# Edge network of one graph layer: the smallest kind of edges multiplied edge by edge in float32 on weights as loaded, placed between the two larger kinds; the second gathered row added one tile behind

## The chip, the core and the metric

The kernel runs on 1 core of one Trainium2 chip. The metric is the time of one execution on the device in microseconds (us). The five engines of the core (TensorE, VectorE, ScalarE, GpSimd, SyncE) run their own instruction lists and meet at semaphores; 16 DMA engines serve all queues of the core.

## What is computed

Two graph layers over 512 nodes with 1024 features, float32. Nearly everything here is in the first one, its edge network:

```python
feat = jnp.concatenate([n_f[edge_src], n_f[edge_dst]], axis=1)      # 8192 edges, 2048 wide
e_hh = jax.nn.relu(feat[:E_HH] @ W_hh + b_hh)                       # 256 edges
e_oo = jax.nn.relu(feat[E_HH:E_HH + E_OO] @ W_oo + b_oo)            # 1280 edges
e_ho = jax.nn.relu(feat[E_HH + E_OO:] @ W_ho + b_ho)                # 6656 edges
logit = (jnp.concatenate([e_hh, e_oo, e_ho], axis=0) @ W_a + b_a)[:, 0]
...                                                                 # alpha: softmax of logit over the edges of a node
z_f = jax.ops.segment_sum(alpha[:, None] * n_f[edge_src], edge_dst, num_segments=N)
h_new = jax.nn.relu(nf2[:NH] @ W_hn + b_hn)                         # nf2 = [n_f, z_f]
o_new = jax.nn.relu(nf2[NH:] @ W_on + b_on)
```

Here n_f is relu(layernorm(x)). The second layer normalizes again, multiplies by W, and sums over neighbours.

## The kernel before

**Tables and tiles.** A row of `feat @ W` is a sum of two rows: source node times the upper half of W, target node times the lower half. So the kernel does not multiply edges. For each of the three kinds of edges (ho, oo, hh, in this order) it multiplies the 512 node rows by both halves of W and stores the results as tables in DRAM, `tab_a` (upper half) and `tab_b` (lower half, bias added). The 8192 edges form 64 tiles of 128: 52 of kind ho (tiles 0 to 51), 10 of oo (52 to 61), 2 of hh (62, 63). For each tile GpSimd gathers 128 rows of 4 KB from `tab_a` and 128 from `tab_b` by an indirect DMA (512 KB each) into slots of `gath` (8 slots). For odd tiles below 62 the two rows go to two slots and VectorE adds them (L888); for all others the second DMA adds onto the first in SBUF (L307), issued `LAG` = 2 tiles behind the first. VectorE then takes relu, times W_a, and the sum of a row in one pass (L893), which frees the slot: this is `edge(q)`.

**Chunks.** TensorE works in chunks of a [1024 x 512] piece of weights: 8 steps k, in each 4 groups of 128 nodes times 3 passes (L638), because a float32 value is held as a high and a low float32r part (`actT_h`, `actT_l`; `ring_h`, `ring_l`) and high*low, low*high, high*high are summed. Chunks 0 to 3 are W_ho, 4 to 7 W_oo, 8 to 11 W_hh (two column halves n for `tab_a`, then two for `tab_b`), 12 to 15 the upper halves of W_on, W_hn, W_hn, W_on over the nodes they concern (3, 1, 1 and 3 groups). A weight tile is loaded by SyncE into one of 8 places of `raw` once VectorE has used the tile there (L232); ScalarE rounds it to `ring_h` (L435), VectorE subtracts for `ring_l` (L868). After a chunk its four banks go to `stage` and to the table: by ScalarE for `tab_a` (L453), by VectorE with the bias for `tab_b` (L876).

**Work hung between the steps.** (c, k) below is step k of chunk c. In chunks 2 to 5 each step also counts two tiles of edges: VectorE makes two one-hot matrices (L819, L820), TensorE multiplies them (L588) into 512 x 512 counts in banks 0 to 3, which ScalarE copies out (L440) at the end of each kind. From chunk 6 on each step adds the logits of a tile: VectorE makes two one-hots (L910, `logit_onehots`), ScalarE scales one by the three bf16 parts of the logit (L482, three instructions a tile, `logit_parts`), TensorE accumulates (L588, three matmuls a tile). A tile takes one of 4 one-hot slots. `SUM_AT` says at which (c, k) tile q is summed: 7 tiles a chunk in chunks 6 to 11, then 8, 6, 6 and 2. `EDGE_AT` puts `edge(q)` 12 steps earlier. When the last tile of a kind is in, the banks are closed (L611), VectorE reads them (`copy_kind`, L932), and the next kind is opened with a mask (L607). Also on VectorE: the inverse counts (L918, L920) in chunks 8 to 10, and the split of finished logits (L899 to L904).

**After chunk 15** come the row maximum (L1006 to L1008), the exponentials, the row sums, the transposes of the attention matrix, the product for z_f (L624), the lower halves of W_hn and W_on, and the second layer. All of that is the same in both kernels.

## Time and profile before

| | us |
|---|---|
| median of 3 runs | 651.68 (649.97 to 654.79) |
| the profiled execution | 648.16 |
| its span in the profile | 646.0 |
| TensorE busy | 556.7 (86%) |
| VectorE busy | 453.9 (70%) |
| ScalarE busy | 306.2 (47%) |
| GpSimd busy | 173.4 (27%) |
| DMA read from and written to HBM | 123.27 MB, 16.78 MB |

The trace of the profiled execution begins 0 us at the start of the span, and all times below are counted from there. A window view gives, for a stretch of the span, how long each engine was busy and in how many instructions, the clock that TensorE was granted, the share of the time in which the 16 DMA engines had a packet in work (it can come out a little over 1), and GB/s. TensorE's busy time in a dense stream overlaps itself, so the distance between starts, not the duration of one matmul, tells its pace.

### The profile page before, as it was taken

The page shows a single profiled execution, that of the slowest core. Times are in us where ns is not written, and L with a number is a line of the kernel's source. Part 1 is how long each engine was busy: PE and PEld are TensorE (multiplying, and loading weights), DVE is VectorE, ACT ScalarE, POOL GpSimd, SP SyncE. Part 2 cuts the span into 40 slices and gives each one's busy share as a digit, 9 for nine tenths or more (in the row PEclk, how much of TensorE's full clock was granted, in tenths as well). Part 3 has the DMA queues.
Part 4 walks back from the last instruction along what each step waited for, and adds up shares of the span by engine and source line. Part 5 has one row for each costly group of instructions (what it writes and reads, how often), then busy time and mean ns, then how long its engine had stood idle before and what let it go on. Part 6 is the DMA issues. An engine that isn't in the chain of part 4 may idle for free.

```text
span 646.0 us, 8205 instructions
## 1 busy us (share of the span) xinstructions
PE 556.7 (86%) x2376; PEld 409.7 (63%) x2377; DVE 453.9 (70%) x958; ACT 306.2 (47%) x485; POOL 173.4 (27%) x165
## 2 busy tenths in 40 slices
PE   0799999999879997979898997568949999779987
PEld 0688777776636765657575764324738788567865
DVE  6715256677986969999989786676795289783252
ACT  2613312114069996656655564499843182332200
POOL 2000300075364564566655553200030000000000
PEclk9999999999979999999998997888978899979999
DMA  8335453499999999999999999843355075130021
GB/s 326 124 132 172 145 192 136 144 243 380 324 331 343 296 328 339 316 330 349 341 342 303 332 317 339 224 145 111 106 225 198 16 245 185 61 102 29 0 82 49
DMA packets 55973, 140.51 MB, mean 218 GB/s; under 512 B 6274, under 2 KB 6402, under 8 KB 55938
## 3 DMA queue, kind: packets, MB, share of 16 engines
q0 software_dynamic: 20624, 74.98, 37.5%
q1 hardware_dynamic: 27072, 50.34, 22.7%
q10 hardware_dynamic: 8242, 14.75, 6.2%
q8 instruction: 18, 0.29, 0.2%
q14 instruction: 17, 0.14, 0.1%
HBM read 123.27 MB, written 16.78 MB: 217 GB/s over the span
## 4 chain that ended last, share of the span: by engine, by line
PE 51%; DVE 22%; DMA 11%; ACT 7%; issue 6%; POOL 2%; ACTq 1%; DVEq 0%; POOLq 0%
PE ps L638 30%; DMA gath<-tab_b,tabl_i 8%; PE ps L624 6%; PE ps L588 4%; ACT onehot L482 4%; DVE gath L893 4%; PE ps L797 3%; DVE gath L888 3%; PE ps L769 3%; DVE ring_l L868 2%; PE ps L782 2%; DVE onehot L910 2%; DMA gath<-tab_a,tabl_i 2%; ACT ring_h L435 1%; DVE logit_d L932 1%
## 5 line engine op out<-in xcount | busy, mean ns | idle before, releaser
L638 PE MATMUL ps<-ring_h,actT_h 128*128 128x512 f32 x520 | 225.8, 434 | 7.2 <-DVE actT_l L861 5.5
L638 PE MATMUL ps<-ring_h,actT_l 128*128 128x512 f32 x520 | 205.5, 395 | 0.0
L638 PE MATMUL ps<-ring_l,actT_h 128*128 128x512 f32 x520 | 204.9, 394 | 0.0
L482 ACT ACTIVATE onehot<-onehot,lgs 128x512 bf16<-128x512 bf16 x192 | 124.6, 712 | 72.3 <-DVE onehot L910 56.4
L435 ACT CAST ring_h<-raw 128x512 fp32r<-128x512 f32 x176 | 104.0, 616 | 105.9 <-PE ps L638 70.7
L868 DVE TENSOR_TENSOR ring_l<-raw,ring_h 128x512 fp32r<-128x512 f32 x176 | 116.9, 685 | 42.0 <-ACT ring_h L435 42.0
L638 PEld LDWEIGHTS ps<-ring_h,actT_h 128*128 128x128 f32 x520 | 99.6, 191 | 41.4 <-DVE actT_l L861 6.5
L588 PE MATMUL ps<-onehot 128*128 128x512 bf16 x292 | 84.1, 398 | 37.3 <-ACT onehot L482 34.2
L638 PEld LDWEIGHTS ps<-ring_h,actT_l 128*128 128x128 f32 x520 | 98.9, 190 | 22.2
L638 PEld LDWEIGHTS ps<-ring_l,actT_h 128*128 128x128 f32 x520 | 99.5, 191 | 20.1
L293 POOL DMA_INDIRECT gath<-tab_a,tabl_i x64 | 69.6, 1088 | 147.9 <-DVE gath L893 69.0
L893 DVE SCALAR_TENSOR_TENSOR gath<-gath,wa_b 128x1024 f32<-128x1024 f32 x64 | 78.4, 1225 | 27.4 <-DMA gath<-tab_b,tabl_i 24.9
L307 POOL DMA_INDIRECT gath<-tab_b,tabl_i x33 | 58.3, 1767 | 64.8 <-DMA tab_b<-stage 47.0
L588 PEld LDWEIGHTS ps<-onehot 128*128 128x128 bf16 x292 | 21.6, 99 | 82.0 <-issue 70.4
L819 DVE TENSOR_SCALAR onehot<-iota_f,node_f 128x512 bf16<-128x512 f16 x64 | 23.4, 366 | 31.9 <-PE ps L588 31.7
L300 POOL DMA_INDIRECT gath<-tab_b,tabl_i x31 | 34.2, 1103 | 24.2 <-DVE gath L893 18.4
L910 DVE TENSOR_SCALAR onehot<-iota_f,node_f 128x512 bf16<-128x512 f16 x128 | 39.4, 350 | 1.1 <-PE ps L588 0.7
L888 DVE TENSOR_TENSOR gath<-gath 128x1024 f32<-128x1024 f32 x31 | 37.7, 1217 | 0.8 <-DMA gath<-tab_b,tabl_i 0.7
L861 DVE TENSOR_TENSOR actT_l<-ps,actT_h 128x512 fp32r<-128x512 f32 x24 | 16.2, 688 | 29.8 <-ACT actT_h L427 29.7
L427 ACT CAST actT_h<-ps 128x512 fp32r<-128x512 f32 x24 | 13.7, 591 | 44.8 <-PE ps L624 34.7
L453 ACT COPY stage<-ps 128x512 f32<-128x512 f32 x24 | 14.1, 586 | 34.4 <-PE ps L638 27.7
L820 DVE TENSOR_SCALAR onehot<-iota_f,node_f 128x512 bf16<-128x512 f16 x64 | 22.2, 348 | 0.0
(162 smaller groups left out, 503.0 us busy)
## 6 DMA issues: line engine op xcount, KB each, us to landing
raw<-in_L_gnn_W_ho_dram SPq DMA_DIRECT2D x32, 256.0 KB
raw<-in_L_gnn_W_oo_dram SPq DMA_DIRECT2D x32, 256.0 KB
...
```

The lines of the kernel that those rows point to most:

```text
L293: pool.indirect_dma_start(out=gath[:, c % GB, :], out_offset=None, in_=tab_a[0:kinds * N, :], in_offset=bass.IndirectOffsetOnAxis(ap=tabl_ ...
L300: pool.indirect_dma_start(out=gath[:, c % GB, :], out_offset=None, in_=tab_b[0:kinds * N, :], in_offset=bass.IndirectOffsetOnAxis(ap=tabl_ ...
L307: pool.indirect_dma_start(out=gath[:, c % GB, :], out_offset=None, in_=tab_b[0:kinds * N, :], in_offset=bass.IndirectOffsetOnAxis(ap=tabl_ ...
L435: nc.scalar.copy(ring_h[:, k, :], raw[:, k % RAW, :]).then_inc(s_high, 1)
L482: ins = nc.scalar.mul(onehot[:, s, 1 + i, :], onehot[:, s, 1, :], lgs[:, i, q:q + 1])
L588: mm = nc.tensor.matmul(ps[:, bass.ds((lo + j) & 3, 1), :].rearrange("p a n -> p (a n)"), onehot[:, s, 1 + i, j * P:(j + 1) * P], onehot[: ...
L624: mm = nc.tensor.matmul(ps[:, b, :], w, v, start=(i == 0), stop=(i == len(pairs) - 1))
L638: mm = nc.tensor.matmul(ps[:, first + m, :], w, v, start=(k == 0 and i == 0), stop=(k == KT - 1 and i == 2))
L868: nc.vector.tensor_tensor(ring_l[:, k, :], raw[:, k % RAW, :], f32(ring_h[:, k, :]), ALU.subtract).then_inc(s_low, 1)
L888: nc.vector.tensor_tensor(gath[:, c % GB, :], gath[:, c % GB, :], gath[:, d % GB, :], ALU.add).then_inc(s_sum, 1)
L893: nc.vector.scalar_tensor_tensor(out=gath[:, c % GB, :], in0=gath[:, c % GB, :], scalar=0.0, in1=wa_b[:, :], op0=ALU.max, op1=ALU.mult, ac ...
L910: ins = nc.vector.tensor_scalar(onehot[:, SLOT[q], j, :], iota_f[:, :], node_f[:, q, e:e + 1], None, ALU.is_equal)
```

## The change

**The hh kind is multiplied by edges.** `KINDS` and the tables of hh are gone. The relu'd rows are stored to a DRAM array `h_d`; four indirect DMAs gather the 2 x 128 source and 2 x 128 target rows of the hh edges from it into `gath`; inside chunk 0 TensorE transposes them (32 transposes, at steps 5 and 7), ScalarE copies them to `featT` (8 copies), which lies over `hrow`; `hrow` is loaded back from `h_d` in chunk 12. Chunks 4 to 7 are now W_hh: at each step two float32 products [128 edges] x [128 x 512], with the weights read straight from `raw`, without rounding, without low part. Both halves of W_hh add up in one bank, so nothing is stored; VectorE adds the bias and takes relu, W_a and the sum from the bank (`hh_edges`, two instructions for each of 4 banks). `raw` is freed by TensorE in these chunks. Chunks 8 to 11 are W_oo.

**The tables of numbers.** Counts begin a chunk earlier, in chunks 1 to 3 (48 tiles), and the last 16 lie in the steps of chunks 4 and 5. Edges: tiles 0 to 11 in chunks 4 to 7, then one at every step of chunks 8 to 12 (tiles 12 to 51), tiles 52 to 58 (oo) from (13, 4) to (15, 2), and 59 to 61 after the last step. Sums: the two hh tiles in chunk 8, 7 tiles in each of chunks 9 to 11, 16 in chunk 12, 8 in 13, 7 in 14, 7 in 15 from step 3 on, 3 after chunk 15. The hh kind is closed first, then ho, then oo. The inverse counts lie in chunks 7, 8 and 10. The seeds of the inverse counts on ScalarE lie in chunks 6 and 7.

**Smaller ones.** `LAG` is 1. The index arithmetic of the edges (VectorE) and its transposes (TensorE) come before chunk 0's products instead of in and after them.

```diff
+        featT = sb("featT", [P, 2 * KT, E_HH], F32, over="hrow")
...
-        tab_a = nc.dram_tensor("tab_a", [3 * N, D], F32).ap()
-        tab_b = nc.dram_tensor("tab_b", [3 * N, D], F32).ap()
+        tab_a = nc.dram_tensor("tab_a", [2 * N, D], F32).ap()
+        tab_b = nc.dram_tensor("tab_b", [2 * N, D], F32).ap()
+        h_d = nc.dram_tensor("h_d", [N, D], F32).ap()
...
+                if q:
+                    if is_split(q - 1):
+                        sp.wait_ge(s_low, RAW + nth_split(q - 1) * KT + k + 1)
+                    else:
+                        sp.wait_ge(s_slot, KT + (q - 1) * KT + k + 1)
+                sp.dma_start(raw[:, k % RAW, :], w[row + k * P:row + (k + 1) * P, n * FB:(n + 1) * FB]).then_inc(s_raw[k % RAW], 16)
...
+            load_chunk(W_ho, 0, 0, 0)
+            for m in range(NM):
+                sp.wait_ge(s_h, m + 1)
+                sp.dma_start(h_d[m * P:(m + 1) * P, :], hrow[:, m, :]).then_inc(s_hd, 16)
+            load_chunk(W_ho, 0, 1, 1)
+            for n in range(NN):
+                load_chunk(W_ho, D, n, 2 + n)
+            for n in range(NN):
+                for half in range(2):
+                    load_chunk(W_hh, half * D, n, CH_HH + 2 * n + half)
+            for half in range(2):
+                for n in range(NN):
+                    load_chunk(W_oo, half * D, n, CH_OO + 2 * half + n)
...
+                if q == CH_EDGE:
+                    sp.wait_ge(s_hd, 16 * NM)
+                    for m in range(NM):
+                        sp.dma_start(hrow[:, m, :], h_d[m * P:(m + 1) * P, :]).then_inc(s_hrow, 16)
...
+            for i in range(2 * T_HH):
+                pool.indirect_dma_start(out=gath[:, NM + i, :], out_offset=None, in_=h_d[:, :],
+                                        in_offset=bass.IndirectOffsetOnAxis(ap=hh_i[:, i:i + 1], axis=0)).then_inc(s_hg[i], 16)
...
-            LAG = 2
+            LAG = 1
...
-        SUM_AT |= {(12, k): 42 + k for k in range(8)}
+        SUMS_AT |= {(12, k): (21 + 2 * k, 22 + 2 * k) for k in range(KT)}
+        LAST_SUMS = (59, 60, 61)
-        EARLIER = 12
+        EDGES_AT |= {(8 + i, k): (12 + i * KT + k,) for i in range(4) for k in range(KT)}
...
+            def hh_rows(j):
+                act.wait_ge(s_ftp, j + 1)
+                nc.scalar.copy(featT[:, 2 * j:2 * j + 2, :].rearrange("p a b -> p (a b)"), ps[:, j % NM, :]).then_inc(s_ft, 1)
...
+            def hh_transposes(k):
+                if k in (5, 7):
+                    if k == 5:
+                        pe.wait_ge(s_spanok, 1)
+                        for i in range(2 * T_HH):
+                            pe.wait_ge(s_hg[i], 16)
+                    for b in range(NM):
+                        j = b + (0 if k == 5 else NM)
+                        if k == 7:
+                            pe.wait_ge(s_ft, b + 1)
+                        for f in (2 * j, 2 * j + 1):
+                            for t in range(T_HH):
+                                c = f % 2 * E_HH + t * P
+                                mm = nc.tensor.transpose(ps[:, b, c:c + P], gath[:, NM + 2 * t + f // KT, f % KT * P:(f % KT + 1) * P], ident[:, :])
+                        mm.then_inc(s_ftp, 1)
+            def hh_chunk(n, half):
+                q = CH_HH + 2 * n + half
+                for k in range(KT):
+                    pe.wait_ge(s_raw[k], 16 * q + 16)
+                    f = half * KT + k
+                    for t in range(T_HH):
+                        b = NM + 2 * n + t
+                        if half == 0 and k == 0:
+                            pe.wait_ge(s_copied, 4 * NM + 2 * n + t + 1)
+                        mm = nc.tensor.matmul(ps[:, b, :], featT[:, f, t * P:(t + 1) * P], raw[:, k, :], start=(f == 0), stop=(f == 2 * KT - 1))
+                        if f == 2 * KT - 1 and t == 0:
+                            mm.then_inc(s_hhc, 1)
+                    mm.then_inc(s_slot, 1)
+                    later_counts(q, k)
...
+            edge_chunk(0, 0, before=hh_transposes)
+            pe.wait_ge(s_ft, KT)
             open_banks()
-            with pe.Fori(0, 3) as c:
-                edge_chunk(c + FIRST_COUNTS, after=lambda k: count_tiles(c * 2, k))
-            edge_chunk(LAST_COUNTS, after=last_counts)
-            pe.wait_ge(s_ccopy, 3)
-            open_masked(0)
-            with pe.Fori(0, 6) as i:
-                edge_chunk(i + 6, before=lambda k: uniform_sums(i, k))
+            with pe.Fori(0, LOOP_COUNTS) as c:
+                edge_chunk(c + FIRST_COUNTS, c + FIRST_COUNTS, after=lambda k: count_tiles(c * 2, k))
+            reg[0] = codes(48 // G, G)
+            for n in range(NN):
+                for half in range(2):
+                    hh_chunk(n, half)
+            chunk(CH_OO, NM, range(NM), lambda m: pe.wait_ge(s_hhd, m + 1), before=lambda k: sums(SUMS_AT.get((CH_OO, k), ())), counted=True)
+            pe.wait_ge(s_kfree, NM)
+            open_masked(0, 2)
+            with pe.Fori(0, 3) as i:
+                edge_chunk(i + CH_OO + 1, i + 5, before=lambda k: uniform_sums(i, k))
...
+            sums(LAST_SUMS)
...
+            def hh_edges(n):
+                dve.wait_ge(s_bias, 48)
+                for t in range(T_HH):
+                    if t == 0:
+                        dve.wait_ge(s_hhc, n + 1)
+                    else:
+                        chunk_done(dve, CH_HH + 2 * n + 1)
+                    b = NM + 2 * n + t
+                    c = slice(n * FB, (n + 1) * FB)
+                    step(nc.vector.tensor_tensor(ps[:, b, :], ps[:, b, :], bias2[:, 0, c], ALU.add))
+                    nc.vector.scalar_tensor_tensor(out=ps[:, b, :], in0=ps[:, b, :], scalar=0.0, in1=wa_b[:, c],
+                                                   op0=ALU.max, op1=ALU.mult, accum_out=lgh[:, t, n:n + 1]).then_inc(s_hhd, 1)
...
+            for p in LAST_EDGES:
+                edge(p)
+            split_logits(LAST_EDGES[0], TG)
+            for p in LAST_SUMS:
+                logit_onehots(p)
+            copy_kind(1)
```

TensorE's rows where the chunks of W_hh end and chunk 8 begins, in the changed kernel (before, chunks 7 and 8 are both made of rows like the last three, 96 to a chunk); L783 are the float32 products:

```order
L688 MATMUL ps<-zeros_r 128x512 x4
L783 MATMUL ps<-raw,featT 128x512 x32
L719 MATMUL ps<-ring_h,actT_h 128x512
L719 MATMUL ps<-ring_l,actT_h 128x512
L719 MATMUL ps<-ring_h,actT_l 128x512
```

The last two chunks of hh are one uninterrupted row of 32 products (64 in the four chunks), where 384 matmuls stood.

ScalarE's rows in chunk 12 before (L435 rounds a weight tile, L482 scales a one-hot, so three of them are a tile):

```order
L435 CAST ring_h<-raw 128x512
L482 ACTIVATE onehot<-onehot,lgs 128x512 x3
L435 CAST ring_h<-raw 128x512
L482 ACTIVATE onehot<-onehot,lgs 128x512 x3
L461 DMA tab_b<-stage 128x512 x4
L435 CAST ring_h<-raw 128x512
L482 ACTIVATE onehot<-onehot,lgs 128x512 x3
```

The same place in the changed kernel, where L500 is the rounding and L547 the scaling, and, behind the dots, its last rows before the exponentials (L610 splits the node rows):

```order
L500 CAST ring_h<-raw 128x512
L526 DMA tab_b<-stage 128x512 x4
L547 ACTIVATE onehot<-onehot,lgs 128x512 x6
L500 CAST ring_h<-raw 128x512
L547 ACTIVATE onehot<-onehot,lgs 128x512 x6
...
L500 CAST ring_h<-raw 128x512
L547 ACTIVATE onehot<-onehot,lgs 128x512 x6
L500 CAST ring_h<-raw 128x512
L547 ACTIVATE onehot<-onehot,lgs 128x512 x18
L610 CAST hrow_h<-hrow 128x1024 x4
```

In chunk 12 two tiles stand between two roundings instead of one, and behind the last rounding of chunk 15 stand six tiles (x18) before the split of the node rows.

GpSimd's rows in the steady part, before (L293 gathers from `tab_a`, L300 from `tab_b` for a plain tile, L307 adds from `tab_b` onto the slot):

```order
L293 DMA gath<-tab_a,tabl_i 128x1024
L300 DMA gath<-tab_b,tabl_i 128x1024
L293 DMA gath<-tab_a,tabl_i 128x1024
L307 DMA gath<-tab_b,tabl_i 128x1024
```

and in the changed kernel (L343, L350, L357 are the same three):

```order
L343 DMA gath<-tab_a,tabl_i 128x1024 x2
L350 DMA gath<-tab_b,tabl_i 128x1024
L357 DMA gath<-tab_b,tabl_i 128x1024
```

The adding DMA of an even tile no longer waits behind the first gather of the next even tile, but stands ahead of it.

## Rows read from the trace of the kernel before

**Rows 1.** Windows: us, busy us of each engine (instructions), TensorE clock, DMA share, GB/s

```profile
core 0: us, PE busy (x) PEld busy (x) DVE busy (x) ACT busy (x) POOL busy (x), PEclk, DMA share, GB/s
47.90:70.50 22.60, 22.60 (x102) 18.27 (x101) 9.90 (x28) 7.10 (x13) 0.00 (x0) 1.00 0.42 141
97.00:123.00 26.00, 26.00 (x116) 19.19 (x115) 16.33 (x45) 4.87 (x8) 0.00 (x0) 1.00 0.35 119
...
127.60:375.80 248.20, 227.73 (x964) 158.50 (x963) 211.79 (x452) 150.59 (x231) 140.64 (x111) 0.98 1.02 325
375.80:409.10 33.30, 25.29 (x99) 16.77 (x97) 26.10 (x54) 17.70 (x29) 15.07 (x13) 0.90 1.02 317
409.10:433.20 24.10, 15.34 (x52) 7.56 (x50) 17.09 (x45) 17.04 (x29) 2.15 (x1) 0.86 0.57 167
433.20:451.40 18.20, 13.51 (x53) 7.00 (x51) 11.75 (x34) 16.88 (x29) 0.00 (x0) 0.91 0.36 114
451.40:481.40 30.00, 21.16 (x97) 16.16 (x95) 25.90 (x65) 21.32 (x34) 5.37 (x10) 0.89 0.41 141
481.40:646.00 164.60, 146.44 (x640) 120.04 (x640) 93.34 (x142) 44.70 (x71) 0.53 (x1) 0.94 0.30 103
```

**Rows 2.** Page, DMA queues: packets, MB, share of 16 engines over the span

```profile
q0 software_dynamic: 20624, 74.98, 37.5%
q1 hardware_dynamic: 27072, 50.34, 22.7%
q10 hardware_dynamic: 8242, 14.75, 6.2%
```

**Rows 3.** Windows of line L893 alone: two instructions for each edge tile

```profile
127.60:188.40 60.80, 16.12 (x26) 0.97 1.00 315
127.60:375.80 248.20, 65.36 (x106) 0.98 1.02 325
```

**Rows 4.** Chain that ended last, in order of time: start us, us, what

```profile
25.56 22.05 PE ps L638 x96
...
123.72 2.99 DMA tab_b<-stage
...
127.63 2.48 POOL gath L307
...
457.93 2.41 DVE ring_l L868 x4
...
481.45 0.79 PE ps L624
```

**Rows 5.** Groups by line and form: out<-in xcount | busy us, mean ns | idle before

```profile
L482 ACT ACTIVATE onehot<-onehot,lgs 128x512 bf16<-128x512 bf16 x192 | 124.6, 712 | 72.3 <-DVE onehot L910 56.4 <-issue 13.4 <-ACT stage L453 1.2
L868 DVE TENSOR_TENSOR ring_l<-raw,ring_h 128x512 fp32r<-128x512 f32 x176 | 116.9, 685 | 42.0 <-ACT ring_h L435 42.0
L435 ACT CAST ring_h<-raw 128x512 fp32r<-128x512 f32 x176 | 104.0, 616 | 105.9 <-PE ps L638 70.7 <-DVE stage L876 13.7 <-PE ps L769 10.7
L893 DVE SCALAR_TENSOR_TENSOR gath<-gath,wa_b 128x1024 f32<-128x1024 f32 x64 | 78.4, 1225 | 27.4 <-DMA gath<-tab_b,tabl_i 24.9 <-issue 1.3
L910 DVE TENSOR_SCALAR onehot<-iota_f,node_f 128x512 bf16<-128x512 f16 x128 | 39.4, 350 | 1.1 <-PE ps L588 0.7
L888 DVE TENSOR_TENSOR gath<-gath 128x1024 f32<-128x1024 f32 x31 | 37.7, 1217 | 0.8 <-DMA gath<-tab_b,tabl_i 0.7
L918 DVE SCALAR_TENSOR_TENSOR newton<-count_d,logit_d 128x256 f32<-128x256 uint16 x24 | 10.1, 421 | 0.4
L617 PE MATMUL ps<-ident,hrow 128*128 128x128 f32 x32 | 5.4, 346 | 17.5 <-ACT hrow L422 17.5
L473 ACT COPY stage<-ps 128x512 f32<-128x512 f32 x8 | 4.7, 585 | 3.0 <-ACT stage L473 1.6 <-PE ps L638 1.4
L746 PE MATMUL ps<-ones,adj 128*128 128x1 f32 x32 | 3.6, 247 | 0.0
L901 DVE CAST lgp<-lgr 128x7 bf16<-128x7 f32 x18 | 3.5, 193 | 0.6
```

More of the change, by code:

```diff
@@ L162, in gnn_kernel @@
         s_h = sem("h_rows")
+        s_hd = sem("h_stored")
+        s_hrow = sem("h_reloaded")
+        s_hidx = sem("hh_edges_loaded")
+        s_hg = [sem(f"hh_rows_gathered{i}") for i in range(2 * T_HH)]
+        s_ftp = sem("hh_transposed_banks")
+        s_ft = sem("hh_rows_ready")
+        s_hhc = sem("hh_banks_done")
+        s_hhd = sem("hh_banks_read")
         s_norm = sem("h_normed")
@@ L322, in _ @@
                 pool.wait_ge(s_st[i], 32)
+            pool.wait_ge(s_ftp, KT)
             for q in range(FIRST):
@@ L332, in _ @@
             bias(0, b_hh)
-            for q in range(FIRST, ET):
-                if q in (T_HO, T_HO + T_OO):
-                    tables_landed(kinds_of(q))
+            for q in range(FIRST, TG):
+                if q == T_HO:
+                    for p in range(T_HO - LAG, T_HO):
+                        if p not in PLAIN:
+                            gather_add(p, 1)
+                    tables_landed(2)
                 gather_src(q, kinds_of(q))
@@ L625, in product, with chunk @@
                 return mm
-            def chunk(q, first, ms, bank_free=None, before=None, after=None, counted=False):
+            def chunk(q, first, ms, bank_free=None, before=None, after=None, counted=False, nth=None):
                 for k in range(KT):
@@ L644, in chunk, with edge_chunk @@
                         after(k)
-            def edge_chunk(q, before=None, after=None):
-                chunk(q, NM, range(NM), lambda m: pe.wait_ge(s_copied, q * NM + m + 1), before, after, counted=True)
+            def edge_chunk(q, i, before=None, after=None):
+                chunk(q, NM, range(NM), lambda m: pe.wait_ge(s_copied, i * NM + m + 1), before, after, counted=True, nth=i)
             reg = [None]
@@ L727, in _ @@
                     free = lambda m: pe.wait_ge(s_copied, waits[c] + (m if c == 0 else 0))
-                chunk(q + c, NM, ms, free, before=lambda k: last_sums(q + c, k))
+                chunk(q + c, NM, ms, free, before=lambda k: sums(SUMS_AT.get((q + c, k), ())))
+            sums(LAST_SUMS)
             pe.wait_ge(s_kfree, 3 * NM)
```

341 lines of the change are left out of this document (186 added, 155 removed).

## Prediction, made before the changed kernel ran

> **What bounds the kernel now.** I read the windows by stage first. Three stretches differ. Up to 123 us TensorE is dense: a chunk without counts takes 22.6 us, one with 16 counted tiles 26.0 [rows 1]. From 127.6 us, when the last `tab_b` store has landed and GpSimd gathers again [rows 4], to about 409 us the 16 DMA engines are never free: their share is 1.02, at 325 and 317 GB/s [rows 1]. In 127.6 to 375.8 TensorE (228 of 248 us) and VectorE (212) are also nearly full, so a shorter TensorE stretch shows up in the time only as far as the DMA lets it. From 409 us the DMA share falls to 0.57 and 0.36, TensorE works 15.3 of 24.1 and 13.5 of 18.2 us, and ScalarE, with 17.0 and 16.9 us, is the fullest [rows 1]: the scalings of the one-hots pace it. From 481.4 to the end, 164.6 us, nothing is changed [rows 1].
>
> The price of DMA work comes from the queues: a queue's share of 646 us, over its MB. Gathers (q0): 0.375 x 646 = 242 us for 74.98 MB, 3.23 us per MB, so a tile (two 512 KB gathers, 1.05 MB) costs 3.4 us. Weights (q1): 0.227 x 646 / 50.34 = 2.9 per MB, a chunk of 2.1 MB 6.1 us. Stores (q10): 2.7 per MB, a table quarter of 1.05 MB 2.9 us [rows 2]. Test on 127.6 to 375.8: L893 shows 106 instructions, so 53 tiles [rows 3]; 53 x 3.4 + 8 chunks x 6.1 + 8 stores x 2.9 = 180 + 49 + 23 = 252 us against 248.2. The stage is priced by its DMA work.
>
> The Trainium skill ("Trainium Kernel Development and Optimization", Key Constraints) says that the queues of all engines run on the same 16 DMA engines and interleave. By that rule the three terms add up, as the trace shows with 252 against 248.2; by a rule of separate queues the stage would be bound by the gathers' 180 us alone, and TensorE's 228 would lead.
>
> **The change, step by step.** I follow the start of a chunk on TensorE, T0 to T15, and G, the time at which gathers can run freely.
>
> *Chunks 0 to 3.* The 32 transposes of gathered rows are new: 32 of the same form cost 5.4 us [rows 5]. Rows and copies are ready long before steps 5 and 7, since TensorE needs 14 us for five steps, and the store and gather of `h` move 4 MB in a stretch whose DMA share is 0.4 [rows 1]; without that cover some 5 us would show. One more chunk carries counts: 26.0 - 22.6 = 3.4 [rows 1]. The index transposes only change place. So T4 goes from 123.0 to 131.8, and G from 127.6 to 136.4.
>
> *Chunks 4 to 7.* Before, 96 matmuls took 22.05 us, 0.23 each [rows 4]. Now 64 float32 products of 512 columns. No row shows one. The nearest float32 product, L746, is 16 in the program and 32 matmuls in the trace [rows 5], so a product is at least two passes: 2 x 0.23 = 0.46, 29 us in all. From above: each of the two passes over a 4-byte operand twice, 0.92, 59 us; and if the clock halved as well, 118. I take 59, with 3.4 for 16 counts: TensorE could start chunk 8 at 194. On the page "FP8 and Floating Point Precision" (TensorE Precision Notes) the Trainium skill has true float32 in 4 passes, which would give the same 59 us.
>
> But VectorE enters chunk 8 only after edge 11. Before, 13 tiles were done by 188.4, 60.8 us after G [rows 3]; 12 tiles are 3.4 less, 1.5 chunks of weights more (+9, since TensorE is further on) and a store less (-2.9): 200. So even at 29 us for the products T8's work starts at about 200; the price of a product is hidden behind the gathers up to 1.0 us each.
>
> *Chunk 8 on VectorE.* 8 steps of L868 (8 x 0.66), 8 edges (8 x 1.23 + 4 x 1.22), 16 short steps of the inverse counts (16 x 0.42), three one-hot pairs (1.8), two splits of seven short steps (2.7), closing hh, masks and `hh_edges` (some 7) [rows 5]: 38 us, where TensorE has 24. Chunk 9 starts about 240, later than DMA alone would make it (8 x 3.4 + 6.1 = 33 us), but the slots hold over 4 tiles ahead, and the next chunks have less for VectorE (25 to 31) than for the DMA (8 x 3.4 + 6.1 + 2.9 = 36). I let the DMA catch up.
>
> *T12.* Before, 53 tiles were done by 375.8. Now chunk 12 needs 43, so 10 fewer (-34.0), and four table stores fewer (-11.6); weights are the same 8 chunks. 248.2 - 45.6 = 202.6 after G: T12 = 339, against 375.8.
>
> *Chunks 12 to 15.* Here the change gives back. The 36.8 us came partly from putting work off: before, 22 of the 64 sums came after T12 (8, 6, 6, 2), now 41 do (16, 8, 7, 7, 3). Chunk 12: ScalarE 16 x 1.95 + 8 x 0.59 = 36 (L482 124.6 us / 192 x 3; L435 104.0 / 176 [rows 5]), VectorE 34, and the DMA 7 tiles, weights, a store and 2 MB of `hrow` coming back, 24 + 6 + 3 + 7 = 40. I take 39. Before: 33.3. Chunk 13: ScalarE 8 x 1.95 + 4.7 + three copies of L473 with their issues, 3 = 23.4. Before 24.1, with a change of kind in it [rows 1]. Chunk 14: 18.2 for six tiles [rows 1], one more is 20. T15 = 421.
>
> The oo tiles wait for tables stored in chunk 12, step 3. Their store lands some 20 us into chunk 12, ten tiles are 34 us of DMA, and the first is wanted at (13, 4), some 50 us in. That holds with 15 us to spare.
>
> *From T15 to the product of z.* Before 30.0 us (451.4 to 481.4), in which TensorE's chunk 15 lay under the softmax [rows 1]. Now nine oo tiles' sums come behind step 3. VectorE must first close ho (2.5), do two edges (3.6), a split (1.4) and a one-hot: scaling starts 8 us in. Seven tiles and four roundings: 24.5. Edges 59 to 61 (6.1) and the last split end about 25; three more scalings, 31.5; accumulate, close and read the banks, 35.6. From there the row maximum and the softmax run exposed: 457.93 to 481.45 less the 2.41 of L868 in it, 21.1 us [rows 4]. Together 57: the product of z starts at 478, against 481.4. The 164.6 us behind it are unchanged: span 643.
>
> *LAG.* GpSimd waits for a first row sooner, with fewer transfers behind it. With plain tiles between, three gathers are still under way, 5 us. I cost it at nothing; if the DMA went idle 0.3 us for each of 26 added tiles, 8 us.
>
> **Sum.** 646.0 + 8.8 - 45.6 + 5.7 (chunk 12) - 0.7 + 1.8 + 27.0 = 643.0, a gain of 3. The profiled execution took 2.2 more than its span, and the median of the three runs is 3.5 above that execution, so I add 5.7: 649 us against 651.7. A change of under 1% (6.5 us) can't be told from none in this kernel.
>
> **Rivals.**
> *Faster (0.32).* The DMA yields more than the mean price, or the tail overlaps better. If chunks 9 to 11 run at the pace that VectorE and TensorE set (about 30 us each from T9 = 240), T12 is 330; and if TensorE's and ScalarE's work in 12 to 15 packs as densely as in the sums above without my waits at the end (4 us), the span is 630, the median 636. For it: before, the DMA and TensorE were both full in this stretch, so it isn't certain which led. Against: the DMA sum closes to 4 us.
> *Slower (0.26).* The tail of the sums. 41 tiles now stand behind T12, with four one-hot slots between three engines. I took 2.4 us a tile in chunk 12. In chunk 14 before, six tiles took 18.2 us, 3.0 each, and in chunk 13, with a change of kind, 24.1, 4.0 each [rows 1]. At 3.0 chunk 12 takes 48 us, 9 more, and a change of kind at (15, 3) priced like that of chunk 13 (24.1 - 18.2) some 5: span 657, median 663. It decides from about 10 us above my sum. Against it: both of those chunks had only one tile a step, with VectorE and TensorE waiting in between.
> *The gain as the products suggest it.* On TensorE alone, 384 matmuls (88 us) become 59: 29 less 8.8, span 626, median 632. For it stands that TensorE was 92% busy there; against it the DMA share. It is in the 0.32.
>
> **How the numbers follow.** My forecast has 0.42: its own errors leave 0.28 within 1%, 0.08 faster, 0.06 slower; its own range is 642 to 656. Of the slower rival's 0.26, 0.06 would end within 1%, of the faster one's 0.32 nothing. So faster 0.32 + 0.08 = 0.40, within 1% 0.28 + 0.06 = 0.34, slower 0.06 + 0.20 = 0.26. The range reaches to the faster rival's 632 and most of the way to the slower's 663: 631 to 663. The product's upper bound, 1.84 us, would put T8 at 253 and end some 30 us later; the clock was 0.98 in this stage [rows 1], so I leave it outside.
>
> **What would show it.** Right: chunk 4's start at 132, hh products 0.9 us apart, VectorE's edge 11 near 200, chunk 12 near 339, chunk 15 near 421, DMA share about 1 from 136 to 360, the z product at 478. Wrong: a DMA share well under 1 in chunks 9 to 11, float32 products over 1.0 us, TensorE waiting at (0, 5) for the gathered rows, or oo gathers landing after VectorE reaches (13, 4).

## The result, and the profile after

The changed kernel takes 671.98 us (median of 4, 669.57 to 674.17) against 650.83 for the kernel before (median of 4, 648.63 to 654.79): a ratio of 1.033 (1.029 to 1.038). The forecast was 649, with a range up to 663. The profiled execution took 673.66 us, with a span of 671.5.

The windows of the changed kernel, cut at the starts of chunks on TensorE: chunks 0 to 3, 4 to 7, then 8, 9, 10, 11, 12, 13, 14, 15 up to the product of z, and the rest. They answer to [rows 1]; the columns are the same.

```profile
core 0: us, PE busy (x) PEld busy (x) DVE busy (x) ACT busy (x) POOL busy (x), PEclk, DMA share, GB/s
25.90:135.20 109.30, 106.92 (x475) 80.78 (x478) 53.43 (x146) 25.32 (x45) 8.27 (x9) 0.98 0.43 152
135.20:204.60 69.40, 62.92 (x165) 27.67 (x164) 38.01 (x79) 30.66 (x30) 32.77 (x27) 0.99 0.99 315
204.60:249.50 44.90, 33.09 (x115) 23.50 (x118) 42.79 (x96) 8.80 (x15) 23.48 (x20) 0.79 0.91 279
249.50:283.20 33.70, 29.77 (x128) 20.18 (x127) 22.07 (x45) 19.67 (x33) 18.20 (x14) 1.00 1.00 304
283.20:325.10 41.90, 30.47 (x120) 20.32 (x118) 34.27 (x72) 20.57 (x34) 20.70 (x17) 0.93 0.98 307
325.10:370.10 45.00, 34.02 (x131) 22.54 (x130) 28.94 (x59) 20.79 (x35) 20.87 (x17) 0.84 0.96 306
370.10:407.50 37.40, 31.48 (x127) 18.85 (x127) 29.76 (x68) 30.11 (x51) 20.57 (x16) 0.95 0.94 281
407.50:430.50 23.00, 14.19 (x50) 7.34 (x49) 14.53 (x36) 20.99 (x36) 8.12 (x7) 0.85 0.99 313
430.50:448.00 17.50, 11.45 (x48) 6.34 (x47) 12.04 (x25) 15.28 (x26) 7.57 (x6) 1.00 0.94 291
448.00:507.50 59.50, 33.11 (x125) 20.45 (x125) 47.07 (x126) 39.60 (x63) 5.37 (x10) 0.77 0.30 93
507.50:671.50 164.00, 145.90 (x640) 119.75 (x640) 93.16 (x142) 44.70 (x71) 0.53 (x1) 0.94 0.30 100
```

In chunks 10 and 11 no engine is full, and in 9 only nearly TensorE: TensorE has 30 of 34, 30 of 42 and 34 of 45 us, VectorE 22, 34 and 29. The DMA share reads 0.96 to 1.00, but it moves only 304 to 307 GB/s, where the kernel before moved 325 with a share of 1.02 [rows 1]. So a high share doesn't say that the transfers were as fast as they can be.

Against the forecast, starts on TensorE in us:

| | chunk 4 | chunk 8 | chunk 9 | chunk 12 | chunk 15 | z product | end |
|---|---|---|---|---|---|---|---|
| before | 123.0 | | | 375.8 | 451.4 | 481.4 | 646.0 |
| forecast | 131.8 | 200 (VectorE) | 240 | 339 | 421 | 478 | 643 |
| after | 135.2 | 204.6 | 249.5 | 370.1 | 448.0 | 507.5 | 671.5 |

Of the 28.5 us that the span is over the forecast, 31.1 are there when chunk 12 starts. Behind it the forecast had 304 us and the trace has 301.4.

What GpSimd waits for says what happened. The list of waits of the changed kernel (engine and line, what it waited for: us in all, times, longest):

```profile
POOL gath L357 <- DMA gath<-tab_a,tabl_i: 102.6, 27, 6.9
DVE gath L1017 <- DMA gath<-tab_b,tabl_i: 57.6, 18, 8.5
POOL gath L350 <- DVE gath L1017: 19.7, 7, 6.0
POOL gath L343 <- DVE gath L1017: 9.7, 3, 3.6
```

and the same waits of GpSimd in the kernel before (L307 is the adding DMA, L293 a first row):

```profile
POOL gath L293 <- DVE gath L893: 69.0, 25, 5.8
POOL gath L307 <- DMA gath<-tab_a,tabl_i: 9.1, 4, 3.6
```

Before, GpSimd waited for VectorE to free a slot (69 us); the DMA share stayed at 1.02 through it [rows 1], so that wait cost nothing that the windows show. Now it waits 102.6 us for a first row to land before it may issue the DMA that adds the second. The queue behind it stands still. The chain that ended last goes through just this. From 140 to 370 us it consists of (DVEq is VectorE's sequencer):

```profile
by line: DMA gath<-tab_a,tabl_i 72.4%; POOL gath L357 17.9%; issue 5.5%; DMA gath<-tab_b,tabl_i 3.8%; DVE gath L1017 0.5%; DVE gath L1012 0.5%; DVEq L1011 0.0%
```

In the kernel before, awaited rows of `tab_a` are 4.3% of the chain from 127 to 375 us. No line of TensorE is in the chain of the changed kernel there, so its lower clock in chunks 8, 10 and 11 (0.79, 0.93 and 0.84 in the windows above) is not what sets the pace. A stretch of that chain in chunks 8 and 9, in order of time (start us, us, what):

```profile
229.27 8.13 DMA gath<-tab_a,tabl_i
237.41 0.26 issue
237.67 1.71 POOL gath L357
239.37 0.30 issue
239.68 6.17 DMA gath<-tab_a,tabl_i
245.84 0.26 issue
246.10 1.56 POOL gath L357
247.66 0.30 issue
247.97 8.15 DMA gath<-tab_a,tabl_i
256.12 0.26 issue
256.38 2.33 POOL gath L357
258.70 0.30 issue
```

A first row of an even tile is issued, lands 6 to 8 us later, the adding DMA takes GpSimd about 2 us, and only then comes the next even tile's first row. One turn serves two tiles. From 229.27 to 259.01 there are three turns, 9.9 us each. The window of L1017 alone, from the first gathers to chunk 12 (columns: us, VectorE busy in it, clock, DMA share, GB/s), shows 45 tiles in 229.5 us, so 10.2 for two:

```profile
140.60:370.10 229.50, 55.49 (x90) 0.91 0.98 305
```

Before, 53 tiles took 248.2 us [rows 3], 9.4 for two. In GpSimd's order at LAG 1 only two gathers stand between the awaited first row and the wait for it, the two of the plain tile. At LAG 2 the first row of the next even tile is issued as well before GpSimd waits, so two such landings overlap. The loop of landing and issuing has become slower than the transfers themselves, and so it sets the pace. The Trainium skill ("DMA: Bandwidth & Descriptors", Anatomy of one DMA — SWDGE (gpsimd) path) says that DMA engines never wait on semaphores and that a wait is served on the issuing sequencer before dispatch. The trace agrees: the 102.6 us stand on GpSimd, and every later gather stands behind them.

### The profile page after: what moved, and what is told of

It reads as the page before. It is cut to its first block, busy times and chain, and to the rows that moved or that the text cites. A ratio compares the mean times of both kernels' runs of the same rounds, so it can differ in the third digit from the quotient of the medians.

```text
span 671.5 us, 7269 instructions
## 1 busy us (share of the span) xinstructions
PE 539.8 (80%) x2144; PEld 373.8 (56%) x2153; DVE 434.0 (65%) x926; ACT 287.9 (43%) x453; POOL 172.2 (26%) x165
## 4 chain that ended last, share of the span: by engine, by line
PE 41%; DMA 29%; DVE 11%; POOL 7%; ACT 6%; issue 5%; ACTq 0%; POOLq 0%; DVEq 0%
DMA gath<-tab_a,tabl_i 26%; PE ps L719 21%; POOL gath L357 7%; PE ps L705 6%; PE ps L665 4%; ACT onehot L547 3%; PE ps L908 3%; PE ps L880 2%; DMA gath<-tab_b,tabl_i 2%; PE ps L893 2%; DVE gath L1017 1%; DVE logit_d L1163 1%; DVE gath L1012 1%; DVE stats L949 1%; ACT ring_h L500 1%
## 5 line engine op out<-in xcount | busy, mean ns | idle before, releaser
L719 PE MATMUL ps<-ring_h,actT_h 128*128 128x512 f32 x392 | 176.3, 450 | 18.8 <-DVE ring_l L992 6.7
L547 ACT ACTIVATE onehot<-onehot,lgs 128x512 bf16<-128x512 bf16 x192 | 123.0, 710 | 112.4 <-DVE onehot L1052 110.8
L719 PE MATMUL ps<-ring_l,actT_h 128*128 128x512 f32 x392 | 158.8, 405 | 0.0
L719 PE MATMUL ps<-ring_h,actT_l 128*128 128x512 f32 x392 | 158.4, 404 | 0.0
L992 DVE TENSOR_TENSOR ring_l<-raw,ring_h 128x512 fp32r<-128x512 f32 x144 | 95.9, 686 | 55.1 <-ACT ring_h L500 54.9
L500 ACT CAST ring_h<-raw 128x512 fp32r<-128x512 f32 x144 | 85.0, 615 | 89.9 <-PE ps L719 54.7
L1017 DVE SCALAR_TENSOR_TENSOR gath<-gath,wa_b 128x1024 f32<-128x1024 f32 x62 | 75.8, 1224 | 58.6 <-DMA gath<-tab_b,tabl_i 57.6
L719 PEld LDWEIGHTS ps<-ring_h,actT_h 128*128 128x128 f32 x392 | 77.4, 197 | 48.2 <-DVE ring_l L992 8.5
L357 POOL DMA_INDIRECT gath<-tab_b,tabl_i x31 | 59.6, 1923 | 149.6 <-DMA gath<-tab_a,tabl_i 102.6
L719 PEld LDWEIGHTS ps<-ring_h,actT_l 128*128 128x128 f32 x392 | 77.2, 197 | 17.7
L719 PEld LDWEIGHTS ps<-ring_l,actT_h 128*128 128x128 f32 x392 | 77.7, 198 | 15.4
L343 POOL DMA_INDIRECT gath<-tab_a,tabl_i x62 | 64.7, 1043 | 83.7 <-DMA tab_a<-stage 56.4
L665 PEld LDWEIGHTS ps<-onehot 128*128 128x128 bf16 x292 | 22.7, 101 | 108.9 <-issue 98.0
L783 PE MATMUL ps<-raw,featT 128*128 128x512 f32 x128 | 56.7, 592 | 0.0
L930 DVE TENSOR_SCALAR onehot<-iota_f,node_f 128x512 bf16<-128x512 f16 x64 | 22.8, 357 | 39.8 <-PE ps L665 39.8
L1052 DVE TENSOR_SCALAR onehot<-iota_f,node_f 128x512 bf16<-128x512 f16 x128 | 38.8, 352 | 2.3 <-PE ps L665 2.1
L783 PEld LDWEIGHTS ps<-raw,featT 128*128 128x128 f32 x128 | 24.3, 190 | 27.3 <-issue 26.0
L350 POOL DMA_INDIRECT gath<-tab_b,tabl_i x31 | 32.1, 1035 | 27.1 <-DVE gath L1017 19.7
```

Source lines behind the costliest of these rows:

```text
L343: pool.indirect_dma_start(out=gath[:, c % GB, :], out_offset=None, in_=tab_a[0:kinds * N, :], in_offset=bass.IndirectOffsetOnAxis(ap=tabl_ ...
L357: pool.indirect_dma_start(out=gath[:, c % GB, :], out_offset=None, in_=tab_b[0:kinds * N, :], in_offset=bass.IndirectOffsetOnAxis(ap=tabl_ ...
L500: nc.scalar.copy(ring_h[:, k, :], raw[:, k % RAW, :]).then_inc(s_high, 1)
L547: ins = nc.scalar.mul(onehot[:, s, 1 + i, :], onehot[:, s, 1, :], lgs[:, i, q:q + 1])
L665: mm = nc.tensor.matmul(ps[:, bass.ds((lo + j) & 3, 1), :].rearrange("p a n -> p (a n)"), onehot[:, s, 1 + i, j * P:(j + 1) * P], onehot[: ...
L719: mm = nc.tensor.matmul(ps[:, first + m, :], w, v, start=(k == 0 and i == 0), stop=(k == KT - 1 and i == 2))
```

## The experiments

All ratios are to runs of the kernel before on the same chip, with their 95% interval.

### The lag alone, in both kernels

`a_lag2` is the changed kernel with the old lag, `b_lag1` the kernel before with the new one.

```diff
-            LAG = 1
+            LAG = 2
```

> The changed kernel with LAG back at 2, everything else as changed. Theory L (the lag): in the changed kernel GpSimd stood 102.6 us behind first rows that had not landed, and the DMA share fell from 1.02 to 0.98 and to 0.91 in chunk 8; with LAG 2 that wait falls under 20 us, chunk 12 starts at 340 to 350 instead of 370, and the time is 645 to 655 us against 650.8 before. Rival W (VectorE's 43 us in chunk 8 and the handoffs of TensorE and ScalarE keep the slots full, so that GpSimd only waits elsewhere): the wait moves to slots not free, chunk 12 stays at 365 or later, and the time stays within 5 us of 672.

> The kernel before with LAG 1 alone. Theory L: GpSimd waits for first rows (over 60 us, 9.1 before), the DMA share of the stretch from 127.6 us falls below 1, and the time rises by 12 to 25 us. Rival W: the lag does no harm where slots are what is waited for, and the time stays within 4 us of 650.8.

`a_lag2`: 658.57 us, ratio 1.011 (1.007 to 1.016). `b_lag1`: 673.54 us, ratio 1.033 (1.027 to 1.039). One tile of lag costs 13.4 us in the changed kernel and 22.7 in the kernel before; there it alone loses as much as the whole change did (21.2). The waits of `b_lag1`, and then its chain by line:

```profile
POOL gath L307 <- DMA gath<-tab_a,tabl_i: 118.5, 28, 6.8
```

```profile
DMA gath<-tab_a,tabl_i 31%; PE ps L638 21%; POOL gath L307 7%; PE ps L624 6%; PE ps L797 3%; ACT onehot L482 3%; PE ps L769 2%; DMA gath<-tab_b,tabl_i 2%; PE ps L782 2%; PE ps L588 2%; DVE logit_d L932 1%; DVE logit_d L1021 1%; ACT ring_h L435 1%; DVE stats L838 1%; DVE hrow_l L1014 1%
```

9.1 us of waiting became 118.5, and the chain now runs for 31% of the span through rows of `tab_a` that are awaited. Its chunk 12 starts at 399.1 instead of 375.8, and from 129 us to there the DMA share is 0.96, at 296 GB/s. This is as theory L had it. In `a_lag2` the waits have gone back to the slots:

```profile
POOL gath L343 <- DVE gath L1017: 65.6, 25, 7.3
POOL gath L350 <- DVE gath L1017: 36.6, 12, 9.6
POOL gath L357 <- DMA gath<-tab_a,tabl_i: 9.7, 6, 3.7
```

From the start of chunk 4 to that of chunk 12 `a_lag2` needs 220.1 us (137.5 to 357.6) and the changed kernel 234.9. So 14.8 of the 31.1 us are the lag. The other 16 are not, and `a_lag2` is outside both expectations: the wait fell to 9.7 us, as theory L had it, but chunk 12 starts at 357.6, not 340 to 350, and the time is above 655 us.

### More lag

```diff
-            LAG = 1
+            LAG = 3
```

> The changed kernel with LAG 3. Theory L: once GpSimd no longer stands behind landings, more lag buys nothing; within 4 us of LAG 2, perhaps 2 to 5 us slower, since a row is finished later and keeps its slot longer. If the run is over 5 us faster than LAG 2, landings still bound the gathers at LAG 2. Rival W: within 5 us of 672.

706.09 us, ratio 1.085 (1.079 to 1.091), 47.5 us more than LAG 2, where I had expected at most 4 or 5. More lag is no safer. GpSimd's longest wait for a slot, VectorE's wait for second rows (41.8 us at LAG 2), and a piece of GpSimd's timeline (start, us, line, and in brackets the idle time ahead and its end):

```profile
POOL gath L350 <- DVE gath L1017: 122.5, 27, 14.4
DVE gath L1017 <- DMA gath<-tab_b,tabl_i: 92.4, 22, 8.8
```

```profile
262.15 0.97 POOL L343 DMA_INDIRECT gath<-tab_a,tabl_i  x1 [4.88 <-DVE gath L1017]
263.43 0.96 POOL L343 DMA_INDIRECT gath<-tab_a,tabl_i  x1 [0.30 <-issue]
266.03 1.07 POOL L350 DMA_INDIRECT gath<-tab_b,tabl_i  x1 [1.64 <-DVE gath L1017]
267.41 2.05 POOL L357 DMA_INDIRECT gath<-tab_b,tabl_i  x1 [0.30 <-issue]
```

Each adding DMA (L357) stands right behind the second row of a later plain tile (L350), which needs a free slot. With 8 slots and three for every two tiles, the second row of tile q takes the slot of tile q - 5. When that slot comes free, VectorE has one finished tile left (q - 4); the next, q - 3, still lacks its second row, and at LAG 3 its adding DMA is only now issued. So GpSimd waits for VectorE and then VectorE for the landing, as the two waits show. The stretch from chunk 4 to 12 (134.4 to 400.4) moves 272 GB/s with a share of 0.90. Of the three values tried, 2 is the best: at 1 the landing is waited for, at 3 the slots.

### Is the price of the float32 products hidden?

`a_lag2_half` is `a_lag2` without 28 of the 64 products.

```diff
+                        if t == 0 and 0 < f < 2 * KT - 1:
+                            continue
```

> LAG 2, and of the 64 float32 products of hh 28 are left out (all but the first and the last of the first tile's sum in each column half). A product took 0.885 us in the changed kernel, so TensorE saves 25 us in chunks 4 to 7. If the products are hidden behind the gathers, as the prediction has it, the time is within 4 us of LAG 2. If TensorE's way to chunk 8 counts, it is 10 to 25 us less.

657.98 us, against 658.57 with all products. 28 products less are 24 us of TensorE, and 0.6 us of time. From the start of chunk 4 to that of chunk 8 it is 66.4 us in both (133.4 to 199.8, 137.5 to 203.9). TensorE doesn't set it; the forecast had said that the gathers do. What a product takes is in TensorE's timeline of the changed kernel (start, us, line, count of matmuls):

```profile
150.29 1.88 PE L783 MATMUL ps<-raw,featT 128*128 128x512 f32 x4
```

Four matmuls, the last 0.59 us long, so (1.88 - 0.59) / 3 = 0.43 from one to the next. A product is two of them, 0.86 us. The forecast chose 0.92.

### The adding DMA against two plain rows

In `a_lag2_plain` every tile from 5 on is plain: 28 adding DMAs become plain gathers into a slot of their own, and VectorE adds. `a_lag1_plain` is the same with `LAG` at 1. In the program, though, `LAG` moves only adding DMAs of tiles from 5 on, and neither kernel has any: both issue the same instructions in the same order.

```diff
-        PLAIN = [q for q in range(T_HO + T_OO) if q % 2]
+        PLAIN = [q for q in range(T_HO + T_OO) if q % 2 or q >= 6]
```

> The changed kernel with LAG 2 in which every tile from 5 on is plain: two gathers into two slots and an addition on VectorE, instead of an adding DMA for the even ones. With LAG 2 (658.6 us) the DMA share was 1.02 from 142 to 358 us, and in the trace's packet records a 4 KB packet of an adding gather takes 0.33 us and a plain one 0.16. Theory: the DMA engines' time sets chunk 12's start (357.6), and an adding row costs two plain ones; 28 tiles at 1.34 us (128 packets x 0.168 / 16) less would be up to 37 us, of which VectorE (1.2 us more a tile, it had 43 of 47 us in chunk 8 and 32 of 37 in chunk 10) takes back 10 to 20: 638 to 648 us. Rival: slots set it; a plain tile takes two of the 8 slots, only four tiles are in flight and VectorE is the pace: 660 to 680 us.

> The changed kernel as it is, LAG 1, but with every tile from 5 on plain, so that nothing waits for a first row behind which it lies (but tiles 2 and 4). Theory: LAG 1 costs what it costs because GpSimd waits at the adding DMA for the first row to land (103 us of waits, while the DMA falls to 305 GB/s); without adding DMAs LAG is nothing, and the time is that of the plain kernel with LAG 2, 651 us within 2, 21 less than with LAG 1 and adding DMAs. Rival: LAG 1 hurts otherwise, by the order of the requests alone: 660 us or more.

650.84 us (ratio 1.001, 0.997 to 1.004) and 651.61 us (1.002, 0.999 to 1.004). That they agree follows from this, so `a_lag1_plain` tests nothing of the lag, and its rival (the order of the requests alone) could not have shown. What the two give is how well one program repeats: 0.8 us in the median, and 212.4 against 211.3 us from chunk 4 to chunk 12. The cause rests on `a_lag2` and `b_lag1`, on the waits and on the chain. The order of the requests changes together with the wait there, and no run separates the two.

The plain kernel beats `a_lag2` by 8 us. The queue of the gathers, in `a_lag2` and in `a_lag2_plain` (packets, MB, share of 16 engines over the span):

```profile
q0 software_dynamic: 20624, 74.98, 36.3%
```

```profile
q0 software_dynamic: 20624, 74.98, 32.9%
```

The same bytes take 0.363 x 657.1 = 238.5 us and 0.329 x 646.6 = 212.7: a gather that is added on its way in costs the DMA engines 0.92 us more than a plain one. The same sum over the other pairs (the changed kernel and `a_lag1_plain`, `a_lag2_inv` and `a_plain_inv`, the kernel before and `b_plain`, `b_inv` and `b_plain_inv`) gives 1.2, 1.1, 0.8 and 1.1 us, so it is about 1 us. The 1.34 of the expectation was too much. The Trainium skill ("Collectives: The Full Stack", Stop ④ — SDMA + CCE: where bytes move and the add happens) says that the addition in the data path is free but that such a transfer is read, read, write. The trace agrees in so far as an adding gather costs more than a copied one, and gives the size. The time is above the 638 to 648 us expected: the DMA has less to do, and now VectorE is nearly full. Windows of `a_lag2_plain`, chunks 8 to 12:

```profile
196.10:243.80 47.70, 31.39 (x117) 22.03 (x118) 46.11 (x94) 12.00 (x20) 17.01 (x17) 0.85 0.85 291
243.80:275.50 31.70, 30.26 (x128) 21.55 (x127) 31.08 (x60) 20.74 (x35) 20.93 (x18) 0.95 0.99 378
275.50:311.40 35.90, 28.38 (x119) 19.58 (x117) 34.94 (x68) 19.78 (x33) 17.21 (x17) 0.96 0.94 319
311.40:345.10 33.70, 31.52 (x130) 21.94 (x130) 33.18 (x63) 20.84 (x35) 19.32 (x17) 0.94 0.96 360
345.10:379.70 34.60, 29.42 (x126) 17.57 (x127) 33.37 (x71) 29.87 (x51) 17.30 (x14) 1.00 0.98 367
```

VectorE (third pair of numbers) is busy 46 of 48, 31 of 32, 35 of 36, 33 of 34 and 33 of 35 us.

### Some tiles plain, and the sums spread

`a_lag2_mix` makes plain 16 more tiles, those whose additions fall where VectorE has room; `b_mix` does so in the kernel before; `a_mix_spread` takes 10 sums in each of chunks 9 to 12 instead of 7, 7, 7 and 16.

```diff
+        PLAIN = [q for q in range(T_HO + T_OO) if q % 2 or q in (6, 8, 10, 20, 22, 24, 26, 36, 38, 40, 42) or q >= T_HO]
...
+        SUMS_AT |= {(9 + i, k): tuple(i * 10 + t for t in TEN[k]) for i in range(4) for k in range(KT)}
```

> The changed kernel with LAG 2 in which 16 more tiles are plain, those whose additions fall where VectorE has room: 6, 8, 10 (34 of 62 us busy in chunks 4 to 7), 20 to 26 (23 of 32 in chunk 9), 36 to 42 (29 of 38 in chunk 11) and the five even oo tiles. DMA theory: 11 tiles before chunk 12 at 1.34 us bring its start from 357.6 to about 343, and the time from 658.6 to about 642 (638 to 646). Slot theory: 655 to 665. If neither the price nor the slots matter, 658.

> The kernel before with the same 16 tiles made plain. Its VectorE was busy 212 of 248 us while the DMA was full. If the DMA alone led there, 11 x 1.34 = 15 us less: about 637. If VectorE led with it, half of that or nothing: 644 to 652; above that if the slots pace it.

> As a_lag2_mix, and the sums spread: 10 tiles in each of chunks 9 to 12 instead of 7, 7, 7 and 16, then 8 and 4, oo as before. If TensorE and ScalarE set the pace of chunks 12 to 14, chunk 12 falls from 36 to about 32 us and chunk 14 from 23 to about 20: some 6 us less than a_lag2_mix. If the DMA engines pace everything up to the last gather, chunks 9 to 11 keep their length and the time is that of a_lag2_mix within 3 us.

658.79 us (ratio 1.013), 653.27 (1.005) and 654.58 (1.008). The mix gave nothing, where the DMA theory had 16 us; `a_lag2_mix` lies in the range of the slot theory, and `b_mix` above both of its theories, where I had put the slots. In chunk 8 of `a_lag2_mix` the DMA fell idle:

```profile
232.00:244.00 12.00, 6.38 (x28) 4.61 (x27) 11.59 (x30) 1.57 (x3) 3.03 (x3) 0.85 0.53 180
```

VectorE is busy almost throughout (11.6 of 12 us), but with closing hh and the inverse counts, and finishes one tile in that time; GpSimd waits 6.7 us for its slot, and the DMA share is 0.53. Why this outweighs the cheaper rows in the mix and not in the kernel with all tiles plain I can't say from these runs. The spread gave 4.2 us, between its two theories. All of it lies behind the start of chunk 12: from there to chunk 15 the trace has 66.8 us instead of 75.2, while chunks 4 to 11 took 221.7 instead of 219.4.

### The work of VectorE in chunk 8

In the remaining runs the inverse counts of ho and oo go from chunks 8 and 10 to 13 and 14, where VectorE has room: 32 instructions of 0.42 us. `a_lag2_inv` does it on `a_lag2`, `a_plain_inv` on `a_lag2_plain`, `a_plain_inv_spread` with the sums spread as above.

```diff
-            INVERSE_AT |= {(8 + 2 * t, 2 * k + 1): (t, k) for t in range(2) for k in range(NM)}
+            INVERSE_AT |= {(13 + t, (1 + t) * k + t): (t, k) for t in range(2) for k in range(NM)}
```

> The changed kernel with LAG 2 and the inverse counts of ho and oo moved from chunks 8 and 10 to chunks 13 and 14: 32 instructions of 0.42 us, 6.7 us less for VectorE in each of chunks 8 and 10. VectorE was busy 43.4 of the 46.8 us of chunk 8, the DMA share 0.92 there and 1.02 to 1.04 behind it. DMA theory: only the idle share comes back, 4 us, and chunk 12 starts at about 354 instead of 357.6; 654 to 657 in all. Rival, VectorE in chunk 8 is a loss that stays: chunk 12 starts 7 to 13 us earlier, 646 to 651.

> The same move on the plain kernel with LAG 2 (650.8 us), in which VectorE is busy 46.1 of 47.7, 31.1 of 31.7, 34.9 of 35.9 and 33.2 of 33.7 us in chunks 8 to 11 and the DMA share is 0.85 to 0.99. VectorE theory: chunk 12 starts up to 13 us earlier, limited by the DMA to about 9 to 12 (345 to about 335); chunks 13 and 14 (VectorE 15.5 of 22.9 and 14.4 of 17.6) give back 3 to 4: 641 to 645 us, faster than both kernels. If something else paces these chunks: 650.

> As a_plain_inv, with the sums spread, 10 tiles in each of chunks 9 to 12. With the mixed kernel the spreading gave 4.2 us, though the DMA share was 0.95 to 1.01 there. Where VectorE paces, nine tiles' one-hots (0.7 us each, 6 us) come ahead of chunk 12 and are saved behind it; chunks 12 and 14 lose their two sums a step: 636 to 642 us. If VectorE is as full in chunks 12 and 13, the time is that of a_plain_inv.

`a_lag2_inv`: 652.42 us, 6.1 less than `a_lag2`, between the two theories. Chunk 4 to 12 takes 212.9 us (135.2 to 348.1) instead of 220.1, 7.2 less, the lower end of what VectorE's theory had. In chunk 8 the DMA is full again (0.99 instead of 0.92; VectorE 37 of 43 us instead of 43 of 47):

```profile
201.80:244.90 43.10, 31.85 (x116) 22.30 (x118) 36.72 (x80) 11.52 (x20) 23.82 (x20) 0.83 0.99 314
```

`a_plain_inv`: 641.38 us, ratio 0.984 (0.979 to 0.988), 1.6% faster than the kernel before and 4.6% faster than the changed one. It is the version that beats both. Its chunks 8 to 11 take 40.9, 31.8, 28.5 and 33.6 us; the third of them moves 393 GB/s:

```profile
270.60:299.10 28.50, 27.13 (x119) 19.54 (x117) 28.02 (x54) 19.63 (x33) 18.17 (x17) 1.00 1.03 393
```

Here VectorE, TensorE and the DMA are all full. The spread on top of it (641.67 us) gives nothing, as its expectation had it for a VectorE that is as full in chunks 12 and 13.

### The same mendings in the kernel before

```diff
-            INVERSE_AT = dict(zip([(c, k) for c in range(8, 11) for k in (1, 3, 5, 7)],
+            INVERSE_AT = dict(zip([(c, k) for c, ks in ((8, (1, 3, 5, 7)), (13, (4, 5, 6, 7)), (14, (2, 3, 4, 5))) for k in ks],
```

> The kernel before, with every tile from 5 to 61 plain. In its full stretch (127.6 to 375.8) VectorE was busy 212 of 248 us; some 24 more additions of 1.22 us there make 241. VectorE theory: it becomes the pace, the stretch stays at 245 to 255 us although the DMA has 0.92 us less for each of the tiles: 648 to 656 us. DMA theory: 22 us less, 630.

> The kernel before, with the inverse counts of oo and hh in chunks 13 and 14 instead of 9 and 10 (those of ho stay in chunk 8, since that kind closes in chunk 13): 32 instructions of 0.42 us, 13.4 us less for VectorE in the full stretch, whose DMA share was 1.02. DMA theory: no gain, 650 within 3. VectorE theory: up to 10 us faster, 640 to 645.

> Both in the kernel before. VectorE has 241 - 13 = 228 us in the full stretch, the DMA some 226, TensorE 228: all three near each other. If the rest of the change is worth nothing, this is level with the changed kernel so mended, 641.4 us. If the shorter TensorE and VectorE work of the products by edges (384 matmuls, 32 splits less) is a gain once GpSimd does not wait, it stays above: 643 to 650.

`b_plain` 652.42 us (ratio 1.003), `b_inv` 654.91 (1.008), `b_plain_inv` 645.00 (0.992, 0.989 to 0.995). The full stretch of the three, in this order, each up to the start of chunk 12:

```profile
129.40:383.90 254.50, 230.51 (x966) 161.28 (x964) 240.55 (x476) 151.63 (x231) 123.19 (x110) 0.96 0.92 319
```

```profile
127.60:376.20 248.60, 229.89 (x964) 160.57 (x963) 199.47 (x420) 150.56 (x231) 135.54 (x111) 0.97 1.01 325
```

```profile
129.20:369.50 240.30, 225.03 (x966) 158.50 (x964) 227.48 (x444) 150.92 (x231) 122.76 (x110) 0.99 0.95 338
```

In `b_inv` VectorE has 12 us less to do (199.5 against 211.8 [rows 1]) and the stretch takes 248.6 us against 248.2, with the DMA share at 1.01: VectorE doesn't lead there. The run is 4 us slower, which lies behind chunk 12, and just outside the 650 within 3 of its DMA theory. In `b_plain` the DMA has less to do, VectorE is at 240.6 of 254.5 us, and nothing is gained. In this kernel only both together help. Each kernel mended in the same way, the changed one takes 641.4 us and the one before 645.0, with ratios whose intervals just part (0.979 to 0.988 and 0.989 to 0.995). So the change without its lag is worth some 3.6 us with both mendings. That is a difference of two medians, of 4 and 5 runs on different chips; two medians of one program were 0.8 us apart above.

## Why the prediction was wrong, point by point

**What failed is the step LAG.** It was "I cost it at nothing", with 8 us as the upper end. It is 14.8 us between chunks 4 and 12 and 13.4 in the median, enough to carry the time past the range: at LAG 2 it is 658.6. My argument was that three gathers are still under way when GpSimd waits, so that the DMA stays fed. That counts the transfers in the DMA engines and leaves out the loop: nothing is issued until the row has landed (6 to 8 us under load) and the adding DMA is issued (2 us), and in this loop there is one even and one odd tile. It also counts one gather too many: two stand behind the awaited row, 3.4 us at my price, and it is three only with that row itself. 8.1 + 0.3 + 1.7 + 0.3 is 10.4 us for two tiles, more than the 6.8 that I priced them at and, with weights and stores on the same engines, more than the 9.4 that they took in all. The trace of before had such landings, one of them in the chain that ended last (start us, us, what):

```profile
141.18 10.58 DMA gath<-tab_a,tabl_i
```

A landing of that size against 3 to 5 us of gathers behind it would have told me that the cover is too short. Nor did I weigh that GpSimd there was waiting 69 us for slots. I take it that rows landed meanwhile, which no run shows by itself; in `b_lag1` that wait is gone (0.7 us) and the one for the landing, 118.5 us, stands in its place.

**Chunk 12 at 339 against 370.1** comes apart so: 3.4 us from chunk 4 (below); 6.8 because I counted 43 tiles up to chunk 12, ten fewer than before, where the window shows 45 (the edges have got one step into chunk 12, as before, so it is eight fewer); 7.2 for the inverse counts that keep VectorE from the tiles (220.1 less 212.9); 14.8 for the lag. That is 32.2 of 31.1. The closeness is partly luck: each part comes from single traces, and the traces of the changed kernel and its variants, alike up to chunk 4, start that chunk anywhere from 133.4 to 137.5 us. Put the other way, my 207.2 us for chunks 4 to 11 with the two tiles more is 214.0, and `a_lag2_inv` took 212.9: the DMA sum holds where neither GpSimd nor VectorE is in its way.

**Chunk 8 on VectorE**, "38 us", was 42.8 busy and 44.9 long. In it are 24 short steps of inverse counts instead of 16 (those of chunk 7 had slid into it) and nine edges instead of eight. "I let the DMA catch up" was wrong as well: the share fell to 0.91 in that chunk. In `a_lag2` it was 0.92 there and 1.02 to 1.04 in the three chunks behind, and yet taking VectorE's inverse counts out (`a_lag2_inv`) brought 7.2 us: the later chunks had not made the loss good.

**Chunks 0 to 3**: chunk 4 starts at 135.2 instead of 131.8. Chunk 0 took 27.7 us, as forecast (22.6 + 5.4), but chunk 1 28.2 instead of 26.0, its first step alone 5.3, and chunks 2 and 3 together 1.4 more. In `a_lag2` TensorE also waited at step 5 of chunk 0 for the gathered rows to land, 2.2 us long, and chunk 4 started at 137.5. `a_plain_inv` and `a_lag3` waited there too, 1.8 and 0.5 us, and the other changed kernels did not: the margin that I had claimed for this landing is about nil.

**The products**: 0.86 us against 0.92 (55 us for the 64 against 59), and hidden, as told. **Right in the tail**: chunk 12 37.4 (39), 13 23.0 (23.4), 14 17.5 (20), from 15 to the product of z 59.5 (57), the rest 164.0 (164.6). The slower rival, that the tail of the sums takes 3 us a tile, did not come: what made the kernel slower lies ahead of the tail.

**The change itself**, apart from the lag, was put at a gain of 3 us. Mended alike, the kernels are 3.6 apart, but that agreement is no proof of the sum, since both are then other kernels than the ones forecast. As written, with VectorE's work in chunk 8, it is 7.7 behind (`a_lag2` 658.6 against 650.9 of the same runs), so without the lag too it would have been 9.6 us above the forecast, though inside its range.
